# An attention and expert block on one core: the front stage rewritten, the transposed rows no longer stored, the routing put into the first units

## The reference

```python
xn = _layernorm(x)
# attention, 16 heads of 64
q, k, v = xn @ Wq, xn @ Wk, xn @ Wv
wei = softmax(where(causal, q @ k.T * 64 ** -0.5, -inf))
attn = (wei @ v).reshape(B, T, -1) @ Wo + bo
# router: two experts a row
r = sigmoid(xn @ gate_w + gate_b)
values, indices = top_k(r, k=2); values /= sum(values)
mlp = lambda x, wg, wu, wd: (silu(x @ wg) * (x @ wu)) @ wd
out = x + attn + xn + mlp(xn, *shared) + sum(values * mlp(xn, *experts[indices]))
```

## Time and profile before

| | us |
|---|---|
| median of 3 runs | 2040.12 (2039.69 to 2041.51) |
| the profiled execution's own time | 2039.6 |
| its span, first to last instruction | 2037.9 |
| PE busy in the span | 1892.4 (93%) |
| DVE busy | 1409.7 (69%) |
| ACT busy | 1205.8 (59%) |
| POOL busy | 1018.4 (50%) |

### The profile page before, as it was taken

The page is one execution under the profiler, slowest core; times in us unless marked ns, Lnnn a source line. Parts: engine busy times, 40 slices in busy tenths (PEclk is TensorE's granted clock), DMA queues, the critical chain, the costliest instruction groups (busy, mean ns, idle before and its releaser), DMA issues.

```text
span 2037.9 us, 53480 instructions
## 1 busy us (share of the span) xinstructions
PE 1892.4 (93%) x20356; PEld 1720.7 (84%) x20356; DVE 1409.7 (69%) x4091; ACT 1205.8 (59%) x3328; POOL 1018.4 (50%) x1515
## 2 busy tenths in 40 slices
PE   4641999999999999999999999999999999999998
PEld 2430898989888899999999999999999989888897
DVE  4667666666666666666676666667666887888865
ACT  2222666666666566666666666666666666655564
POOL 0004467776766343443433434334343777777752
PEclk9765999999999999999999999999999999999999
DMA  9878243434342354434544345453442334333210
GB/s 273 291 298 338 66 143 123 148 125 147 125 146 90 125 156 135 146 128 148 164 133 156 120 148 154 139 160 118 155 136 69 109 102 118 110 112 103 89 33 12
DMA packets 162196, 284.95 MB, mean 140 GB/s; under 512 B 27552, under 2 KB 113312, under 8 KB 157344
## 3 DMA queue, kind: packets, MB, share of 16 engines
q1 hardware_dynamic: 135264, 164.16, 25.6%
q0 software_dynamic: 23808, 96.49, 14.4%
q10 hardware_dynamic: 2880, 20.97, 2.5%
HBM read 169.36 MB, written 112.20 MB: 138 GB/s over the span
## 4 chain that ended last, share of the span: by engine, by line
PE 70%; POOL 11%; issue 6%; ACT 1%; DVE 1%; DMA 0%; POOLq 0%; SPq 0%; DVEq 0%
PE d_bank L811 14%; PE d_bank L863 11%; PE d_bank L849 10%; PE d_bank L838 9%; PE d_bank L824 7%; POOL d_probs L1307 7%; PE d_bank L879 7%; PE d_bank L917 6%; POOL queued_rows L1270 4%; PE d_bank L904 3%; PE d_bank L895 2%; PE d_bank L927 1%; ACT d_probs L980 1%; PE d_bank L884 1%; POOL d_base L1261 1%
## 5 line engine op out<-in xcount | busy, mean ns | idle before, releaser
L1307 POOL TENSOR_SCALAR d_probs<-d_probs,d_inverse 128x512 f32<-128x512 f32 (+3 forms) x1024 | 546.6, 549 | 740.5 <-DVE d_inverse L1104 738.9
L980 ACT ACTIVATE d_probs<-d_probs,d_bias 128x512 f32<-128x512 f32 (+3 forms) x1024 | 561.0, 552 | 1.2 <-DVE d_bias L1098 1.2
L811 PE MATMUL d_bank<-d_xnt,wqk_all 128*128 128x512 f32 x1536 | 414.8, 406 | 41.1 <-DMA d_xnt<-xnt_split 41.1
L1098 DVE CUSTOM_DVE_ANT_0 d_probs<-d_bank,mask 128x512 f32<-128x512 f32 (+3 forms) x1024 | 439.0, 485 | 1.9 <-PE d_bank L849 1.8
L811 PEld LDWEIGHTS d_bank<-d_xnt,wqk_all 128*128 128x128 f32 x1536 | 274.3, 190 | 96.5 <-DMA d_xnt<-xnt_split 42.0
L849 PE MATMUL d_bank<-d_ks,d_qs 64*128 64x512 f32 (+3 forms) x3072 | 313.1, 333 | 8.7 <-issue 6.8
L863 PE MATMUL d_bank<-d_probs_t,d_v 128*64 128x128 f32 x5120 | 310.3, 276 | 0.0
L973 ACT ACTIVATE d_probs_t<-d_bank 128x512 f32<-128x512 f32 (+1 forms) x384 | 188.9, 526 | 205.1 <-PE d_bank L838 205.0
L863 PEld LDWEIGHTS d_bank<-d_probs_t,d_v 128*64 128x64 f32 x5120 | 279.2, 138 | 15.8 <-issue 3.8
L849 PEld LDWEIGHTS d_bank<-d_ks,d_qs 64*128 64x128 f32 x3072 | 250.4, 186 | 27.9 <-issue 10.9
L838 PE MATMUL d_bank<-ident_r,d_probs_moved 64*128 64x64 f32 x5120 | 255.8, 244 | 9.4 <-POOL d_probs L1307 9.3
(11 more groups left out here) (126 smaller groups left out, 2258.9 us busy)
## 6 DMA issues: line engine op xcount, KB each, us to landing
queued_rows<-a_zeros ACTq DMA_DIRECT2D x20, 1024.0 KB, 17.4
d_x<-queued_rows SPq DMA_DIRECT2D x80, 256.0 KB, 3.8
routed_rows<-d_y SPq DMA_DIRECT2D x80, 256.0 KB, 4.2
xnt_split<-a_xnt SPq DMA_DIRECT2D x16, 1024.0 KB, 4.2
d_xnt<-xnt_split SPq DMA_DIRECT2D x64, 256.0 KB, 3.6
expert_rows<-d_w SPq DMA_DIRECT2D x32, 384.0 KB, 3.5
a_x_in<-in_L_attn_x SPq DMA_DIRECT2D x16, 512.0 KB, 4.9
xn_rows<-a_xn SPq DMA_DIRECT2D x16, 512.0 KB, 5.5
```

The lines of the kernel that those rows point to most:

```text
L811: last = pe.matmul(to[:, :], wqk[:, n % PAIRS, "qk".index(kind), wa, k, :], xnt[n // PAIRS % 2][:, xb, k, :], start=first, stop=(k == KD - ...
L980: act.activation(part, part, ACT.Exp, bias=bias[:, i, h:h + 1], scale=-1.0, accum_out=total[which][:, at % 4:at % 4 + 1]).then_inc(exp_don ...
L1098: dve.tensor_tensor_reduce(out=probs[:, i, h, 0:cols], in0=bank(f"s{fill}", u, h)[:, at * P:at * P + cols], in1=mask[:, T - cols:T], scale ...
L1307: pool.tensor_scalar(part, part, inverse[which][:, at % 4:at % 4 + 1], 1.0, ALU.mult, ALU.mult).then_inc(norm_done, 1)
```

## The change

In the front, xn has four buffers instead of two, and the transposed rows are not split and not stored. PE transposes xn as fp32r (a second name, `turned`, for the same memory), ACT copies the result whole, and PE makes the logits from it with the rows as the stationary operand, so that they come out by rows and need no second transpose. The loops are written out. The weights are loaded one tile behind each batch's store, and ACT and POOL split them two batches later.

In the stream, SP loads xn of a batch (`normal`, now the whole batch), and in one step of each batch (u = -3, 3, 11, 19, ...) PE transposes it (`turn`), ACT copies the high parts and DVE subtracts the low parts (`split_normal`) into `d_xnt`.

The routing is cut into ten pieces, `route(u)`, each the last thing that DVE does in steps 0 to 9; PE's counting matmuls (`count`) are in steps 4 and 6. The clearing of `queued` goes to SP in steps 0 to 9, in 80 transfers of 256 KB. The scatter begins at step 10 instead of 2, the packs at 12, and the slot passes at step 46 with two ticks in every step, so that they end with step 86. Many tiles share one region of 32 KB a partition (`flex`), and y has one buffer instead of two.

```diff
-FIRST_SCATTER = 2
+ZERO_COLS = 512
+FLEX_AT = 229344 - 32 * 1024
+FIRST_SCATTER = 10
...
+        DEEP = 4
...
+                def load_x(b):
+                    if b >= DEEP:
+                        sp.wait_ge(xn_done, b - DEEP + 1)
+                    sp.dma_start(x_in[b % DEEP][:, :, :], x_src[b]).then_inc(x_loaded[b % DEEP], DMA)
+                def store(b):
+                    sp.wait_ge(xn_done, b + 1)
+                    sp.dma_start(dram["xn"][b], xn[b % DEEP][:, :, :]).then_inc(xn_stored[b % DEEP], DMA)
...
+                for b in range(B):
+                    store(b)
+                    if b < len(loads):
+                        sp.dma_start(loads[b][1], loads[b][0]).then_inc(stage_loaded[b], DMA)
+                    if b + DEEP < B:
+                        load_x(b + DEEP)
...
-                def store(b, r, more):
-                    wait_apart(sp, xn_done, START + b + 1, begun)
-                    if more:
-                        load_x(b + 2, r)
-                    sp.dma_start(dram["xn"][bass.ds(b, 1)].rearrange("b p q d -> (b p) q d"), xn[r][:, :, :]
-                                 ).then_inc(xn_stored[r], DMA)
-                    wait_apart(sp, lo_done, START + b * KD + KD, begun)
-                    sp.dma_start(dram["xnt"][bass.ds(b, 1)].rearrange("b p n -> (b p) n"),
-                                 xnt[r][:, :, :, :].rearrange("p a k t -> p (a k t)").bitcast(F32)
-                                 ).then_inc(xnt_stored[r], DMA)
...
+                deviation(0)
+                for b in range(B):
+                    if b + 1 < B:
+                        deviation(b + 1)
+                    take_xt(b)
+                    if 2 <= b < 2 + len(loads):
+                        split(b - 2)
...
+                moments(0)
+                for b in range(B):
+                    if b + 1 < B:
+                        moments(b + 1)
+                    normalise(b)
+                    if b >= 2:
+                        take_logits(b - 2)
...
-                def split_xt(b, r):
-                    for k in range(KD):
-                        dve.wait_ge(hi_done, b * KD + k + 1)
-                        dve.tensor_tensor(xnt[r][:, LO, k, :], xt_ps[r][:, k, :], xnt[r][:, HI, k, :].bitcast(F32),
-                                          ALU.subtract).then_inc(lo_done, 1)
...
+                def transposes(b):
+                    pe.wait_ge(xn_done, b + 1)
+                    if b >= 2:
+                        pe.wait_ge(xt_out, (b - 1) * KD)
+                    for k in range(KD):
+                        for q in range(QT):
+                            last = pe.transpose(xt_ps[b % 2][:, k, q * P:(q + 1) * P].bitcast(F32R),
+                                                turned[b % DEEP][:, q, k * P:(k + 1) * P], keep["ident_r"][:, :])
+                        last.then_inc(xt_ready, 1)
...
+                            last = pe.matmul(lg_ps[b % 2][:, q, 0:E], xt[b % 2][:, k, q * P:(q + 1) * P], gate_w[:, k, :],
+                                             start=(k == 0), stop=(k == KD - 1))
+                    last.then_inc(lg_ready, 1)
...
         FILL = {3: 0, 1: 1, 20: 2}
         PARTS = {3: ((3, 0),), 1: ((1, 0),), 20: ((2, 0), (0, 3))}
         SCATTER_AT = {FIRST_SCATTER + n: (n // 2, n % 2) for n in range(2 * B)}
-        PACK_AT = {2 * e + 2: e for e in range(E)}
-        FIRST_TICK = FIRST_SCATTER + 2 * B + 1
-        TICKS, at = {}, [(u, part) for u in range(FIRST_TICK, UNITS) for part in range(2) if part or u % 2 == 0]
+        PACK_AT = {FIRST_SCATTER + 2 + 2 * e: e for e in range(E)}
+        SUMS_AT, RANKS_AT = 4, 6
+        ZERO_PARTS = SLOTS * D // (P * ZERO_COLS)
+        FIRST_TICK = FIRST_SCATTER + 2 * B + 4
+        TICKS, at = {}, [(u, part) for u in range(FIRST_TICK, UNITS) for part in range(2) ]
         for n in range(SLOT_TILES + 2):
...
+                def clear(n):
+                    rows_of = P * ZERO_COLS // D
+                    sp.dma_start(dram["queued"][n * rows_of:(n + 1) * rows_of, :].rearrange("(p q) d -> p (q d)", p=P),
+                                 zeros[:, :]).then_inc(zero_stored, DMA)
...
                 def store_y(t):
                     sp.wait_ge(y_done, t + 1)
                     sp.dma_start(dram["routed"][t * SLOT_TILE:(t + 1) * SLOT_TILE, :].rearrange("(s p) d -> p s d", p=P),
-                                 y[t % 2][:, :, :]).then_inc(y_stored[t % 2], DMA)
+                                 y[:, :, :]).then_inc(y_stored, DMA)
...
+                        if 0 <= u < ZERO_PARTS // 8:
+                            for n in range(2):
+                                clear(u * 8 + slot * 2 + n)
+                        if u in (FIRST_SCATTER - 1, FIRST_SCATTER):
+                            s = u - FIRST_SCATTER + 1
+                            load_rows(s, slot)
...
-                        if k == PAIRS - 2 and b >= 0 and b + 2 < B:
-                            if slot == 0:
-                                sp.wait_ge(p_ready, 2 * PAIRS * (b + 1))
-                                sp.wait_ge(v_ready, PAIRS * (b + 1))
-                            load_xnt(b + 2, slot // 2, slot % 2)
...
-                        if k == 4 and 0 <= b < B - 1 and slot == 2:
-                            load_normal(b + 1, 0)
-                        if k == PAIRS - 1 and 0 <= b < B - 1 and slot == 2:
-                            load_normal(b + 1, 1)
+                        if k == 2 and 0 <= b < B - 1 and slot >= 2:
+                            load_normal(b + 1, slot - 2)
...
+                def turn(u):
+                    b = (u + 5) // PAIRS if u > 0 else 0
+                    pe.wait_ge(normal_loaded, (b + 1) * 2 * DMA)
+                    for k in range(KD):
+                        to = take(f"n{k}", u)
+                        for q in range(QT):
+                            last = pe.transpose(to[:, q * P:(q + 1) * P].bitcast(F32R), normal[:, q, k * P:(k + 1) * P],
+                                                ident[:, :])
+                        last.then_inc(n_ready, 1)
...
+                def count(kind, u):
+                    flat = both[:, :, :].rearrange("p t e -> p (t e)")
+                    pe.wait_ge(both_ready, 1)
+                    for n in range(2):
+                        last = pe.matmul(take(f"{kind}{n}", u)[:, :], (ones_b if kind == "sum" else before)[:, :],
+                                         flat[:, n * T:(n + 1) * T], start=True, stop=True)
+                    last.then_inc(sums_ready if kind == "sum" else ranks_ready, 1)
...
                 def take_y(t):
                     act.wait_ge(y_ready, t + 1)
-                    if t >= 2:
-                        act.wait_ge(y_stored[t % 2], t // 2 * DMA)
-                    act.activation(y[t % 2][:, :, :].rearrange("p s d -> p (s d)"), bank("dn", t)[:, :], ACT.Copy
+                    if t:
+                        act.wait_ge(y_stored, t * DMA)
+                    act.activation(y[:, :, :].rearrange("p s d -> p (s d)"), bank("dn", t)[:, :], ACT.Copy
                                    ).then_inc(y_done, 1)
...
+                def split_normal(u):
+                    b = (u + 5) // PAIRS if u > 0 else 0
+                    for k in range(KD):
+                        dve.wait_ge(n_hi, b * KD + k + 1)
+                        dve.tensor_tensor(xnt[b % 2][:, LO, k, :], bank(f"n{k}", u)[:, :], xnt[b % 2][:, HI, k, :].bitcast(F32),
+                                          ALU.subtract).then_inc(n_out, 1)
...
+                def route(u):
+                    if u == 0:
+                        dve.wait_ge(made, 8)
+                        then(dve.tensor_copy(rank_of_e[:, :], small["rank_i"][:, :]))
...
+                        mark_highest(0)
+                    elif u == 1:
+                        choose(0)
+                        then(dve.scalar_tensor_tensor(flat(gates), flat(chosen[0]), -4.0, flat(gates), ALU.mult, ALU.add))
+                        then(dve.tensor_reduce(best[1][:, :], gates[:, :, :], AX.X, ALU.max))
+                    elif u == 2:
+                        mark_ties(1)
+                        choose(1)
...
+                    elif u == SUMS_AT:
+                        dve.wait_ge(sums_ready, 1)
+                        for n in range(2):
+                            dve.tensor_copy(flat(tile_sum)[:, n * T:(n + 1) * T], bank(f"sum{n}", u)[:, :]).then_inc(sums_out, 1)
+                        dve.wait_ge(sums_out, 2)
+                        for e in range(6):
+                            then(dve.tensor_tensor_scan(spots[:, :, e], ones[:, :], tile_sum[:, :, e], 0.0, ALU.mult, ALU.add))
+                    elif u == 5:
+                        for e in range(6, E):
+                            then(dve.tensor_tensor_scan(spots[:, :, e], ones[:, :], tile_sum[:, :, e], 0.0, ALU.mult, ALU.add))
...
+                    elif u == RANKS_AT:
...
+                        dve.wait_ge(ranks_ready, 1)
```

(17 more changed lines are left out.)

593 lines of the change are left out of this document (250 added, 343 removed).

## The result

The changed kernel takes 2061.34 us (median of 4 runs, 2058.73 to 2062.44). The kernel before, on the same chip, takes 2039.9 us (2039.26 to 2041.51). The ratio is 1.0102, with a 95% interval of 1.0085 to 1.012. The forecast was 2009 us, a gain of 1.5%; its range ended at 2042, and slower than before had a chance of 0.12. The profiled execution has 2058.73 us and a span of 2057.0 us, 19.1 us longer than the span before.

The account below looks back on a forecast made before the run. PE was taken to bound the stream, with the front ahead of it; 2037.9 - 99 + 11.5 + 22 + 35 = 2007.4 us of span, 2009 us with 1.7 around it; range 1966 to 2042.

Parts of the forecast that it names:

- above that the excess is PE's wait: Routing in steps 0 to 9: a piece costs nothing up to 2.5 us, the excess is PE's wait; excesses sum to 13 us.
- the loss of a plain step is the landing time less 3.75 us: Slot passes: with one y buffer, a plain step loses the y store's landing time less 3.75 us, taken as 1.15 us.
- front, PE's first projection: Ahead of the stream: PE's first projection at 100 us (bounds 92 and 119) instead of 199.5, gain 99 us.
- turns, 15: Stream: 15 turns of a batch by PE, 0.77 us each, cost 11.5 us (bounds 9 and 25).
- routing: waits of PE, steps 0 to 13: First steps of the stream: routing pieces cost 22 us (bounds 8 and 33).
- slot passes: waits of PE, steps 46 to 84: Slot passes: two ticks a step with one y buffer cost 35 us over 41 steps (bounds 5 and 80).
- The step on the logits: End of the front: logits after the last batch's transposes and copy take about 1 us (bounds 0.4 and 2.9).
- rival (b): Front and routing: DVE is held by POOL and routing pieces are dearer; 2039 us in full, 2026 by half; chance 0.12.
- the 4 us put on the path: Front: POOL's eight subtractions beside DVE's normalising add 4 us to the path, bounds 0 and 23.
- A constant landing of 4.9: Slot passes: y stores taken to land 4.9 us after issue, a little over the median of 4.7.
- (c): Slot passes: y stores land late in every step, slower than before; 2064 us at a landing of 6.5; chance 0.10.
- PE's share of 93 to 95% in the slot passes: Sign for the slot passes: PE's busy share there falls to 93 to 95% instead of 100.

Follow-up runs that it names:

- the doubled work: Changed kernel with PE's transposes and scores ahead of its two short waits run twice in the even steps 48 to 84; 2152.3 us, ratio 1.0167.

## Why the prediction was wrong

Two steps of it failed, and in the same way. The price of a routing piece was "above that the excess is PE's wait", and that of a step with slot passes "the loss of a plain step is the landing time less 3.75 us": both take what PE waits as the whole loss, and put at nothing, without a reason, the slow stretch that follows. The waits came out near the forecast; the clock loss behind them, 18.8 and 37.6 us, stands nowhere in it. Its terms in the order in which it had them, for the spans of the two profiled executions, in us:

| term | forecast | measured |
|---|---|---|
| front, PE's first projection | -99 | -97.5 |
| turns, 15 | +11.5 | +12.0 |
| routing: waits of PE, steps 0 to 13 | +22 | +16.4 |
| routing: clock loss | 0 | +18.8 |
| slot passes: waits of PE, steps 46 to 84 | +35 | +31.3 |
| slot passes: clock loss | 0 | +37.6 |
| sum | -30.5 | +18.6 |

The measured sum is 0.5 us from the difference of the spans, 19.1, but that closeness is in part chance, as the last four rows do not take off what the kernel before has. Counted whole, from PE's first projection to the end, PE's idle time grows from 26.2 to 71.4 us, the clock loss from 16.6 to 68.3 and the rest from 1795.7 to 1815.3: 45.2, 51.7 and 19.6 us. Of the 19.6 the turns are 12.0; the others, PE's counts among them, were not taken apart. The clock loss alone is as large as the distance between forecast and result (50 us in the spans, 52 in the times).

**The front.** The gain is right to 2 us, with the wrong engine as its limit, and in part by luck: the sigmoid ends 5.4 us later than forecast, and 3.4 us of that come back behind it. The step on the logits took "about 1 (bounds 0.4 and 2.9)" for them; they take 3.56 us a batch, and with 1.23 us of transposes PE sets the pace at 4.43 us from 68 us on, not VectorE at 3.9. The bound itself didn't hold. The sigmoid starts at 94.35 us, where the forecast's 90 us had its end. Most of what comes back does so at the stream's start: from SP's load to PE's first turn it is 3.5 us (95.68 to 99.22) and not 6.0.

**The lock between VectorE and GpSimd**, rival (b). VectorE's four normalisations take 1.38 us alone; beside a subtraction of GpSimd:

```profile
26.62 3.41 DVE L251 TENSOR_SCALAR a_xn<-a_x_in,a_mean_var,a_rstd 128x256 f32<-128x256 f32 x4
```

GpSimd's subtraction beside it:

```profile
27.22 2.34 POOL L186 TENSOR_TENSOR wqk_all<-a_staged,wqk_all 128x1024 fp32r<-128x1024 f32 x1 [2.05 <-ACT wqk_all L212]
```

VectorE is held for 2.0 us, nearly the full 2.34, five times so from 26 to 53 us. The rule of the Trainium skill, page "SBUF — State Buffer", section "Who interferes with whom", that the loser of the lock stands for the whole instruction, agrees with these rows. It cost more than the 4 us put on the path. Between its first transposes at 11.25 us and its last logits at 94 us PE waited only for L251, seven times, 10.5 us in all, and 8.6 of these stand behind a normalisation that was held (five of 3.4 us and one of 4.11 beside the subtraction of 4.54). As PE sets the pace, they are on the path, though not all for the lock: in two of the six cases x had come about 0.9 us late. The bound of 23 held.

**The turns** are as forecast: 0.80 us for eight transposes (0.77).

**The routing.** The first failed step: "above that the excess is PE's wait": the waits are 16.4 us (15.0 more than in the same steps before), less than the 22 taken. But each of the four steps with 2.5 us or more of waits also has 3.4 us of clock loss, PE at half its clock for some 7 us (so has step 6, with 0.8 us of waits), and in all that is as dear again; the two together, 35.2 us, are what the stretch costs more than with the routing ahead of it (35.5). The experiment with the finer pieces removes both: 2.3 us of idle and 1.8 of clock loss are left in steps 0 to 13.

**The slot passes.** The second: "the loss of a plain step is the landing time less 3.75 us": for step 54 the store of 901.76 is through by 907.38, 5.6 us, and the formula gives 1.9 us; PE's waits are 1.4. Over the stage PE's waits are 31.3 us against the 35 forecast. But the step lost 4.8 us, 1.4 in waits and 3.4 in the clock. A constant landing of 4.9 was wrong too: the part 1 stores take 5.6 us in one step and 4.0 in the next (923.22 to 927.26), so every other step loses, and strongly, instead of each a little (26.8 of the 31.3 us are in even steps). That the sum of the waits came out near 35 is therefore luck in part. Why they alternate isn't settled. The trace has a hint: nine of the part 1 stores are issued 0.8 to 0.9 us behind a gather of weights by POOL (L1264), and they take 5.4 to 6.4 us; that of 901.76 is one, that of 923.22 stands 3.1 us behind its gather. But others 3.3 us behind one take up to 7.6 us, and no run moved the gathers. That the waits move to the next step when the first is covered speaks against a property of even steps.

**The rivals.** (c) ended on the right side, and its sign of recognition is met (steps 46 to 84 take 19.4 us on average, "over 19"). But its mechanism was a mean landing above 5.9 us, while the median is 3.8 and the mean of the 80 stores 4.1, and the queues were not crowded (146 GB/s). It came about at the landings of the forecast itself. Its chance of 0.10 came from asking whether landings could be that late, and not what else a wait could cost. Of the signs named, PE's share of 93 to 95% in the slot passes was nearly met (761.27 of 795 us, 95.8%): who had looked at that column alone would have called the forecast confirmed. The clock beside it, 0.95, held the other half.

The kernel before could have told it. In the earlier trace rows PE is busy for 1812.2 of 1838.5 us at 0.99; the 1% is some 17 us of clock loss beside 26 us of idle. That ratio was in the row from which the whole sum started, and was not used.

Two sums of the forecast are off by little: the chain from the landing to the probs copy adds up to 4.00 us and not 4.05, and rival (b) by half is 2024 us and not 2026. Neither changes a choice.

## What to carry to other kernels

A wait of a busy PE is priced as idle time plus the slow stretch behind it. Here that was 1.15 and 1.2 us more for each microsecond waited, in the two stages of the changed kernel on the first chip; other runs give 0.7 (the doubled work) to 1.5 (steps 46 to 84 with the finer routing: 31.3 us idle, 46.1 of clock loss), so it is a size and not a rate. Two columns of the windows give both, so read the clock beside the busy share. Before a second buffer is given up, look where the transfer that empties the first is issued: one place in the queue was worth 75 us, more than the memory. Work put into the gaps of another engine has to be cut to the gap, and to the gap in front of the instruction that PE waits for; cut coarser, it comes back almost in full (2 to 5 of 40 us hidden), cut finer it hid 34 (step 14 begins at 308.0 us, and at 341.6 with the routing ahead).

## What the runs showed of the hardware

- Two waits of 0.7 us within 2.4 us were followed by PE rows at half speed for about 6 us (granted clock 0.84 over the step, 1.2 GHz in the stretch). Not each wait was: of steps 46 to 84, 11 have a clock loss, of 1.7 to 5.1 us, and others with as much idle time have none. Step 56 has waits of 0.87 and 0.69 us, and its rows stay at full speed; it is long for the shared MLP's matmuls (3.1 us). What decides between them stays open. The row of step 56:

```profile
943.84:965.67 21.83, 20.27 (x197) 18.24 (x196) 13.51 (x36) 11.41 (x31) 8.64 (x14) 1.00 0.46 148
```

- A matmul over few columns can be dear: 16 records of 128x16 took 3.56 us, 0.22 us each, where 12 of 128x256 take 1.58 us, 0.13 us each. The weight loads of the 16, of 128x128 numbers each, take 3.49 us of the same stretch, so they set the pace. By the code these operands are float32 and those of the 128x256 fp32r; what of the difference is the type and what the load wasn't tried apart.
- A VectorE instruction waits for a GpSimd one beside it: four normalisations of 1.38 us took 3.41 us beside a subtraction of 2.34 us, five times so.
- Two chips ran the kernel before 4% slower than the first, 2120 to 2124 against 2040 us, with a mean granted clock of 0.94 in those runs of the third (0.99 in the stream on the first). The changed kernel shows where: 70 us more in steps 86 to 127 (third chip), of it 30 us of PE's idle time and 35 of clock loss. What PE's waits there come from was not looked into.
